# Token mixer on Trainium2: ranks in two products from a count kept per image, narrower query passes, and the last pair's work in another place

## The chip, the cores and the metric

The kernel runs on one core of one Trainium2 chip. The metric is the device time of one launch in microseconds (us). A core has TensorE (PE; its weight loads are listed as PEld), VectorE (DVE), ScalarE (ACT), GpSimd (POOL) and SyncE (SP), which only issues DMAs. Each runs its own list of instructions in order, and they meet at semaphores.

## The reference, cut to what matters

```python
h = tok(x)                               # 64 images of 3x96x96: 36 patches of 768 numbers -> 256, a class token, positions
h = concatenate([h, txt], axis=1)        # 64 x 114 x 256
# linear attention, 16 heads of 16, no softmax
n = layernorm(h); Q, K, V = n@Wq.T+bq, n@Wk.T+bk, n@Wv.T+bv
Q, K = elu(Q)+1, elu(K)+1
KV = einsum('bshd,bshe->bhde', K, V);  Z = 1/(Q . sum_s K + 1e-6)
h = h + einsum('bshd,bhde,bsh->bshe', Q, KV, Z) @ Wo.T + bo
# top-1 mixture of 8 experts
x = layernorm(h); logits = x @ gate_w.T; sel = argmax(logits); rw = sigmoid(max(logits))
xs = x * rw                              # only the chosen expert e = sel works on a row
h = h + (xs @ w_up[e].T) * silu(xs @ w_gate[e].T) @ w_down[e].T
```

## The kernel before, in words

**Stages.** A start of about 50 us makes the patch rows. Then comes a loop over 32 pairs of images (a pair is two images of 114 tokens, `p` is the pair, `i` the step), in which each engine works on several pairs at once: in step i TensorE makes keys, values and queries of pair i, applies the attention of pair i-1, projects out pair i-2 and ranks pair i-4; VectorE routes pair i-3 and takes the statistics of pair i+2 (`stats_1`) and of pair i-2 (`stats_2`); GpSimd works on the second layer norm of pair i-3 (`rstd2_of`), scatters pair i-4 and works on the first layer norm of pair i+2 (`rstd1_of`). Behind the loop the last pairs are finished among the first tiles of the expert stage: 64 tiles of 128 rows sorted by expert, two at a time (a duo, `Turn(0, m)`, `duo_step`), 32 duos. All orders are written out by hand, in the functions `step` of each engine and in the straight lists behind the loop.

**Numbers in float32.** A product of precise numbers is three passes over a high and a low part of each operand (`product`, lines 1537 to 1539). The query product of a pair is 12 such passes: 2 halves `c` by 2 halves `k` by 3. They are 264 columns wide though only 228 are used, because the bank `b_w` is then seeded with the bias and the 264 columns of the output projection are added on it.

**Ranks.** Every token needs its place in its expert's region. `route` on VectorE makes `chosen`, a 0/1 mask of 114 tokens by 8 experts for each of the two images, and `so_far` holds for each partition the number of choices of all earlier pairs (its last row holds the start of each region). `rank(p)` on TensorE sums with matrices of ones: choices earlier in the image (line 1570), those of the first image for the second (line 1571), and the two halves of `so_far` (line 1573, twice). `count_chosen(p)` on GpSimd adds `chosen` to `so_far`, in two buffers by turns. `rank(p)` thus needs the count up to pair p-1 only. `places` on VectorE masks the ranks, and GpSimd's `scatter` writes the rows, two indirect DMAs a pair, to `sorted_rows`.

**Early table.** Once 23 pairs are counted, TensorE, VectorE and GpSimd work out which expert each of the first 32 tiles has (`early_count`, `early_slots`, `early_ends_out`, `early_share`, and on GpSimd `early_past`, `early_sums`, `early_rows` in steps 28, 29 and 30). The late 32 tiles follow from `late_count` and so on after the last pair.

**GpSimd's queue.** Step i is `rstd2_of(i-3)`, `ids_in(i-3)`, `scatter(i-4)`, `count_chosen(i-3)`, `rstd1_of(i+2)`, `top_value(i-3)`, then in steps 5 to 28 the low part of one expert weight (lines 711 and 716). `scatter` waits for ScalarE's `gains`. ScalarE's `tanh(p)` waits for `top_value(p)`. Behind the loop GpSimd also issues all 64 stores of results (`store`, line 820, one indirect DMA a tile), in the same queue as the last pairs' counts, norms and scatters. A store needs only VectorE's result of its tile (line 1427), and 16 result buffers stand between the two.

Of the kernel before, what the change touches and what calls it, by code (L numbers as in the profile page):

```python
# [115 lines left out]
def build(nc, x, txt, w_tok, pos, wq, bq, wkgv, wo, wo_rows, bias, drop, bias_kv, bo_col, wgu_in, wdown_in, ids, consts, slots, out):  # L116
    scratch = nc.dram_tensor("sorted_rows", (EXPERTS * REGION + P, ROW), F32, kind="Internal").ap()

    with ExitStack() as ctx:
# [515 lines left out]
        def _(pool):  # L635
# [197 lines left out]
            store(Turn(0, 1))  # L833
# [10 lines left out]
        def _(act):  # L844
# [273 lines left out]
        def _(dve):  # L1118
# [157 lines left out]
            def route(p):  # L1276
# [13 lines left out]
                if p >= 2:  # L1290
                    dve.wait_ge(so_far_ready, p - 1)
# [19 lines left out]
            def early_link(ins, count):  # L1311

                ins.then_inc(early_chain, 1)
                dve.wait_ge(early_chain, count)

            def early_count():
# [3 lines left out]
                early_link(V.tensor_scalar(early_i[:, 0:1], early_held, con["c_regcol"][:, 0:1], None, ALU.subtract), 1)  # L1320
                early_link(V.tensor_scalar(early_i[:, 1:2], early_i[:, 0:1], P.bit_length() - 1, None, ALU.logical_shift_right), 2)
# [20 lines left out]
            def step(i):  # L1342
# [6 lines left out]
                if 0 <= i - 4:  # L1349
                    places(i - 4)  # L1350
# [696 lines left out]
```

## Time and profile before

| what | us |
|---|---|
| median of 3 runs (lowest, highest) | 429.08 (428.54, 429.84) |
| the profiled execution, its own time | 429.01 |
| its span, first to last instruction | 427.2 |
| PE busy, weight loads | 403.9, 397.4 |
| DVE, ACT, POOL busy | 353.5, 318.1, 288.1 |
| share of the chain that ended last: PE, POOL | 91%, 2% |
| mean granted TensorE clock | 0.982 of full speed |

The span is the stretch that the profile shows; the launch has 1.8 us around it. "Busy" of an engine is the sum over its instructions. A chain entry gives what the next instruction was waiting for, and where nothing was waited for, the instruction before it on the same engine. A matmul's recorded length overlaps with the next ones, so what one costs is read from the distance of starts or from the lengths in the chain. The rest of this document gives times as us from the span's start.

### The profile page before, as it was taken

What the parts mean: (1) busy time and instruction counts of PE and PEld (TensorE: products, weight loads), DVE (VectorE), ACT (ScalarE), POOL (GpSimd) and SP (SyncE); (2) the same over time, 40 slices, a digit from 0 to 9 for tenths busy, and PEclk for the clock granted to TensorE, in tenths of its full rate; (3) what the DMA queues carried; (4) which work ended last, traced back from release to release, by engine and by line L of the source; (5) the groups of instructions that cost most, each with busy time, mean ns of one, the idle gap of its engine ahead of it and who ended that gap; (6) DMA issues with size and microseconds to landing.
All of it is one profiled execution on the core that took longest, in us unless ns stands there. A gap on an engine that the chain in (4) does not pass through costs nothing.

```text
span 427.2 us, 13531 instructions
## 1 busy us (share of the span) xinstructions
PE 403.9 (95%) x4389; PEld 397.4 (93%) x4389; DVE 353.5 (83%) x1076; ACT 318.1 (74%) x856; POOL 288.1 (67%) x539
## 2 busy tenths in 40 slices
PE   7999999999999999999999999999989999999920
PEld 7999999999999999999999999999989999999910
DVE  5677558999999999999999999998888987777730
ACT  5444477789989988988998898888697877777700
POOL 4065212577788788788878878778757677777772
PEclk9999999999999999999999999999999999999975
DMA  8975121232432131332112112200684469622220
GB/s 282 343 239 165 48 49 48 87 110 71 120 99 66 42 111 51 89 107 57 39 50 61 45 39 64 65 25 24 168 224 144 162 190 295 219 82 90 75 92 15
DMA packets 34151, 46.49 MB, mean 109 GB/s; under 512 B 8842, under 2 KB 25856, under 8 KB 34082
## 3 DMA queue, kind: packets, MB, share of 16 engines
q1 hardware_dynamic: 24860, 30.50, 23.7%
q0 software_dynamic: 9216, 15.12, 11.4%
q8 instruction: 37, 0.61, 0.6%
q14 instruction: 32, 0.26, 0.2%
q10 hardware_dynamic: 6, 0.00, 0.0%
HBM read 26.87 MB, written 17.17 MB: 103 GB/s over the span
## 4 chain that ended last, share of the span: by engine, by line
PE 91%; POOL 2%; issue 2%; DMA 1%; ACT 1%; DVE 1%; POOLq 0%; SPq 0%
PE b_kg L1537 9%; PE b_w L1537 8%; PE b_kg L1539 8%; PE b_kg L1538 8%; PE b_w L1538 8%; PE b_w L1539 8%; PE b_att L1652 7%; PE b_t L1602 4%; PE b_v L1539 3%; PE b_v L1537 3%; PE b_v L1538 3%; PE b_t L1666 3%; PE b_att L1589 3%; PE b_att L1537 3%; PE b_att L1539 2%; PE b_att L1538 2%
## 5 line engine op out<-in xcount | busy, mean ns | idle before, releaser
L702 POOL DMA_INDIRECT sorted_rows<-rows,place x64 | 75.1, 1174 | 41.7 <-ACT rows L887 29.5
L820 POOL DMA_INDIRECT out<-result,rows_all x64 | 66.5, 1039 | 20.2 <-issue 13.1
L956 ACT ACTIVATE q_exp<-b_w,bq_s 128x228 f32<-128x228 f32 x64 | 28.9, 452 | 24.4 <-PE b_w L1539 24.4
L1537 PE MATMUL b_w<-xnT_hi,wq_hi 128*128 128x264 f32 x128 | 39.5, 309 | 0.1
L1537 PE MATMUL b_kg<-wkgv_hi,xnT_hi 128*114 128x264 f32 x128 | 38.7, 302 | 0.4 <-DVE patch_out L1164 0.4
L1063 ACT ACTIVATE silu_g<-b_kg,rows_all 128x128 f32<-128x128 f32 x64 | 23.5, 368 | 20.6 <-PE b_kg L1539 18.7
L1537 PE MATMUL b_kg<-wgu_hi,xsT_hi 128*128 x128 | 36.6, 286 | 0.0
L1538 PE MATMUL b_kg<-wkgv_lo,xnT_hi 128*114 128x264 f32 x128 | 36.4, 285 | 0.0
L1538 PE MATMUL b_w<-xnT_lo,wq_hi 128*128 128x264 f32 x128 | 36.4, 285 | 0.0
L1539 PE MATMUL b_kg<-wkgv_hi,xnT_lo 128*114 128x264 f32 x128 | 36.4, 284 | 0.0
L1539 PE MATMUL b_w<-xnT_hi,wq_lo 128*128 128x264 f32 x128 | 36.4, 284 | 0.0
L1652 PE MATMUL b_att<-kv_sb,qT 128*114 128x136 f32 x256 | 34.9, 279 | 1.3 <-DVE qT L1226 1.3
L1539 PE MATMUL b_v<-wkgv_hi,xnT_lo 128*114 128x256 f32 x128 | 36.1, 282 | 0.0
L1537 PE MATMUL b_v<-wkgv_hi,xnT_hi 128*114 128x256 f32 x128 | 36.0, 281 | 0.0
L1538 PE MATMUL b_kg<-wgu_lo,xsT_hi 128*128 x128 | 35.8, 280 | 0.0
L1538 PE MATMUL b_v<-wkgv_lo,xnT_hi 128*114 128x256 f32 x128 | 35.7, 279 | 0.0
L1538 PE MATMUL b_w<-wo_lo,attnT_hi 128*114 128x264 f32 x124 | 35.2, 284 | 0.0
L1537 PE MATMUL b_w<-wo_hi,attnT_hi 128*114 128x264 f32 x124 | 35.1, 283 | 0.0
L1539 PE MATMUL b_w<-wo_hi,attnT_lo 128*114 128x264 f32 x124 | 35.1, 283 | 0.0
L911 ACT ACTIVATE xn<-rows_all,shift,rstd 114x255 f32<-114x255 f32 x64 | 34.8, 595 | 0.0
L1652 PEld LDWEIGHTS b_att<-kv_sb,qT 128*114 128x114 f32 x256 | 31.7, 178 | 1.5 <-issue 1.5
L901 ACT ACTIVATE rows<-rows,mean_neg 114x256 f32<-114x256 f32 x64 | 29.2, 510 | 0.1
(250 smaller groups left out, 1640.6 us busy)
## 6 DMA issues: line engine op xcount, KB each, us to landing
rows_all<-sorted_rows SPq DMA_DIRECT2D x64, 130.0 KB
rows_all<-in_x SPq DMA_DIRECT2D x18, 384.0 KB, 4.8
rows_all<-in_txt SPq DMA_DIRECT2D x32, 154.0 KB
rows_all<-in_wgu_in SPq DMA_DIRECT2D x8, 256.0 KB, 2.9
rows_all<-patch_out SPq DMA_DIRECT2D x48, 36.0 KB
sorted_rows<-tail_rows SPq DMA_DIRECT2D x9, 130.0 KB, 2.3
sorted_rows<-rows,place POOLq DMA_INDIRECT x64, 3.8
rows_all<-in_wdown_in SPq DMA_DIRECT2D x2, 512.0 KB, 4.6
```

The lines of the kernel that those rows point to most:

```text
L702: G.indirect_dma_start(out=scratch[0:EXPERTS * REGION, :], out_offset=bass.IndirectOffsetOnAxis(ap=place[:, k, b:b + 1], axis=0), in_=rows ...
L820: G.indirect_dma_start(out=out, out_offset=bass.IndirectOffsetOnAxis(ap=rows_all[:, t.n, ID:ID + 1].bitcast(I32), axis=0), in_=result[:, k ...
L901: last = S.activation(rows[:, p % 4, b, 0:D], rows[:, p % 4, b, 0:D], ACT.Identity, bias=mean_neg[:, b:b + 1])
L911: last = S.activation(xn[:, b, 1:], rows_all[0:TOK, 2 * p + b, 1:D], ACT.Identity, bias=shift1[:, p % 8, b:b + 1], scale=rstd1[:, p % 8, b ...
L956: S.activation(q_exp[:, c, :], at, ACT.Exp, bias=bq_s[:, c:c + 1])
L1063: S.activation(silu_g[:, t.slot(4)], bank[:, 0:INNER], ACT.Silu, scale=gain)
L1537: T.matmul(to, left_hi, right_hi, start=start, stop=False, skip_group_check=seeded)
L1538: T.matmul(to, left_hi, right_lo, start=False, stop=False, skip_group_check=seeded)
L1539: return T.matmul(to, left_lo, right_hi, start=False, stop=stop, skip_group_check=seeded)
L1589: last = T.matmul(b_kv[j * PART:(j + 1) * PART, b * KC + c], k_sb[:, b, at:at + PART], v_sb[:, b, c, j, :], start=True, stop=True)
L1602: last = T.transpose(turn_attn_bank(p)[:, at:at + TOK], attn[:, b, c * P:(c + 1) * P], ident[0:TOK, 0:TOK])
L1652: last = T.matmul(b_att[0:TOK, b, c * KVW:(c + 1) * KVW], qT[:, c, b * TOK:(b + 1) * TOK], kv_sb[:, b * KC + c].rearrange("p j w -> p (j w ...
```

## The change

1. `so_far` now holds two running numbers of each expert: the count before the pair, and the count with its first image. `count_chosen(p)` on GpSimd makes the second and then, waiting for it, the count for the next pair: two additions of 8 columns in place of one of 16. `rank(p)` is two products in place of four, and waits for the first addition of its own pair. The products of `early_count` and `late_count` are one in place of two. The constant that fills `so_far` at the start now holds the region starts in both halves.
2. GpSimd's step has another order: norms of both kinds first, then the tile table's last part, the count, the scatter, `top_value`.
3. Ten of the twelve query passes of a pair are 256 columns wide in place of 264.
4. VectorE's small chain for the early table is spread over its step, so that other work stands between its links.
5. Behind the loop: ScalarE takes `tanh` and `gains` of pairs 28, 29 and 31 earlier (and the last pair's ahead of duo 5); VectorE takes `stats_2(31)` ahead of duo 3, not behind duo 4; GpSimd's `scatter(31)` stands ahead of the stores of duo 2, and `rstd2_of(31)` ahead of those of duo 1.

```diff
# gpsimd
             def count_chosen(p):
                 pool.wait_ge(chosen_ready, p + 1)
                 if p >= 1:
+                    pool.wait_ge(so_far_ready, 2 * p)
                     pool.wait_ge(rank_done, p)
-                    pool.wait_ge(so_far_ready, p)
-                G.tensor_tensor(so_far[0:TOK, (p + 1) % 2], so_far[0:TOK, p % 2], chosen[:, p % 2],
-                                ALU.add).then_inc(so_far_ready, 1)
+                now, then = so_far[0:TOK, p % 2], so_far[0:TOK, (p + 1) % 2]
+                G.tensor_tensor(now[:, 1], now[:, 0], chosen[:, p % 2, 0], ALU.add).then_inc(so_far_ready, 1)
+                pool.wait_ge(so_far_ready, 2 * p + 1)
+                G.tensor_tensor(then[:, 0], now[:, 1], chosen[:, p % 2, 1], ALU.add).then_inc(so_far_ready, 1)
...
             def step(i):
+                if 0 <= i - 3:
+                    rstd2_of(i - 3)
+                    ids_in(i - 3)
+                if 0 <= i + 2 < PAIRS:
+                    rstd1_of(i + 2)
                 if i == EARLY_PAIRS + 7:
                     early_rows()
                 if 0 <= i - 3:
-                    rstd2_of(i - 3)
-                    ids_in(i - 3)
+                    count_chosen(i - 3)
                 if 0 <= i - 4:
                     scatter(i - 4)
-                if 0 <= i - 3:
-                    count_chosen(i - 3)
-                if 0 <= i + 2 < PAIRS:
-                    rstd1_of(i + 2)
                 if 0 <= i - 3:
                     top_value(i - 3)
...
             scatter(PAIRS - 2)
-            store(Turn(0, 1))
             rstd2_of(PAIRS - 1)
             ids_in(PAIRS - 1)
             top_value(PAIRS - 1)
-            store(Turn(0, 2))
+            store(Turn(0, 1))
             scatter(PAIRS - 1)
-            for m in range(3, DUOS):
+            for m in range(2, DUOS):
                 store(Turn(0, m))
# scalar, behind the loop
             attention_high(PAIRS - 2)
+            tanh(PAIRS - 4)
             seed_bias(PAIRS - 2)
+            gains(PAIRS - 4)
             rows_high(Turn(0, 0))
-            tanh(PAIRS - 4)
             means(PAIRS - 3)
-            gains(PAIRS - 4)
...
             rows_high(Turn(0, 1))
+            tanh(PAIRS - 3)
             attention_high(PAIRS - 1)
-            tanh(PAIRS - 3)
+            gains(PAIRS - 3)
             gate_and_up(Turn(0, 0))
-            gains(PAIRS - 3)
...
             duo_step(Turn(0, 4))
-            duo_step(Turn(0, 5))
+            tanh(PAIRS - 1)
             means(PAIRS - 1)
             centred(PAIRS - 1)
-            duo_step(Turn(0, 6))
-            tanh(PAIRS - 1)
             gains(PAIRS - 1)
-            straight(range(7, DUOS + 1), duo_step)
+            straight(range(5, DUOS + 1), duo_step)
# vector
+                if i == EARLY_PAIRS + 4:
+                    early_whole()
+                if i == EARLY_PAIRS + 5:
+                    early_share()
                 if 0 <= i - 2:
                     attention_low(i - 2)
-                if i == EARLY_PAIRS + 5:
-                    early_share()
+                if i == EARLY_PAIRS + 4:
+                    early_number()
                 if 0 <= i - 1:
                     queries(i - 1)
+                if i == EARLY_PAIRS + 5:
+                    early_compare()
...
             places(PAIRS - 1)
+            stats_2(PAIRS - 1)
             duo_step(Turn(0, 3))
             late_count()
             duo_step(Turn(0, 4))
             late_ends()
-            stats_2(PAIRS - 1)
# tensor
             def rank(p):
                 pe.wait_ge(chosen_ready, p + 1)
-                if p >= 1:
-                    pe.wait_ge(so_far_ready, p)
+                pe.wait_ge(so_far_ready, 2 * p + 1)
...
                 T.matmul(ranks, earlier[:], chosen[:, p % 2].rearrange("p b e -> p (b e)"), start=True, stop=False)
-                T.matmul(ranks[:, EXPERTS:], ones_bf[0:TOK, :], chosen[:, p % 2, 0, :], start=False, stop=False)
-                for b in range(2):
-                    last = T.matmul(ranks, ones_bf[:, :], so_far[:, p % 2, b:b + 1, :].to_broadcast([P, 2, EXPERTS]),
-                                    start=False, stop=(b == 1))
-                last.then_inc(rank_done, 1)
+                T.matmul(ranks, ones_bf[:, :], so_far[:, p % 2].rearrange("p b e -> p (b e)"), start=False, stop=True).then_inc(rank_done, 1)
...
             def queries(p):
                         w = slice(c * P, (c + 1) * P)
-                        last = product(b_w[:, c, 0:QW], (wq_hi[:, k, w], wq_lo[:, k, w]),
-                                       (xnT_hi[:, p % 2, k, :], xnT_lo[:, p % 2, k, :]), k == 0, k == KC - 1)
+                        width = QW if k == 0 else D
+                        T.matmul(b_w[:, c, 0:width], wq_hi[:, k, w], xnT_hi[:, p % 2, k, 0:width], start=(k == 0), stop=False,
+                                 skip_group_check=True)
+                        T.matmul(b_w[:, c, 0:D], wq_hi[:, k, w], xnT_lo[:, p % 2, k, 0:D], start=False, stop=False, skip_group_check=True)
+                        last = T.matmul(b_w[:, c, 0:D], wq_lo[:, k, w], xnT_hi[:, p % 2, k, 0:D], start=False, stop=(k == KC - 1),
+                                        skip_group_check=True)
```

## Rows read from the trace of the kernel before

**Rows 1.** Windows: twenty steps of the pair loop (us; busy us by engine).
```profile
100.19:265.20 165.01, 165.01 (x2003) 163.62 (x2002) 154.83 (x521) 145.40 (x401) 130.46 (x281) 1.00 0.24 70
```

**Rows 2.** Waits of VectorE, 100 to 300 us (total, times, longest).
```profile
DVE z L1262 <- ACT den L939: 5.6, 22, 0.3
```

**Rows 3.** Timeline of GpSimd, one step (start, length, instruction, idle before it).
```profile
200.71 0.22 POOL L685 TENSOR_TENSOR so_far<-so_far,chosen 114x16 bf16<-114x16 bf16 x1
...
202.79 0.74 POOL L711 TENSOR_TENSOR wgu_lo<-rows_all,wgu_hi 128x256 fp32r<-128x256 f32 x1
...
204.66 0.58 POOL L669 TENSOR_TENSOR ratio<-spread,rstd_half 114x2 f32<-114x2 f32 x1
...
206.29 1.24 POOL L702 DMA_INDIRECT sorted_rows<-rows,place  x1 [0.93 <-ACT rows L887]
```

**Rows 4.** Timelines, last pair: GpSimd with its first stores; VectorE's results of duo 3.
```profile
324.58 1.06 POOL L820 DMA_INDIRECT out<-result,rows_all  x1 [0.75 <-DVE result L1427]
...
334.77 0.27 POOL L664 TENSOR_SCALAR ve<-rows 114x2 f32<-114x2 f32 x1 [2.08 <-DVE rows L1182]
...
342.55 1.00 POOL L820 DMA_INDIRECT out<-result,rows_all  x1 [0.30 <-issue]
...
335.24 0.86 DVE L1427 SCALAR_TENSOR_TENSOR result<-rows_all,b_att 128x256 f32<-128x256 f32 x2
```

**Rows 5.** Timelines, expert stage: VectorE's result of duo 23 and a gate product; GpSimd's stores.
```profile
390.49 0.87 DVE L1427 SCALAR_TENSOR_TENSOR result<-rows_all,b_att 128x256 f32<-128x256 f32 x2
...
395.29 0.43 DVE L1411 TENSOR_TENSOR act_u<-up_g,silu_g 128x256 f32<-128x256 f32 x1 [0.59 <-ACT up_g L1064]
...
395.37 1.20 POOL L820 DMA_INDIRECT out<-result,rows_all  x1 [0.30 <-issue]
396.87 0.97 POOL L820 DMA_INDIRECT out<-result,rows_all  x1 [0.30 <-DVE result L1427]
```

**Rows 6.** Timelines, the end: VectorE's last results, GpSimd's last store.
```profile
408.97 0.87 DVE L1427 SCALAR_TENSOR_TENSOR result<-rows_all,b_att 128x256 f32<-128x256 f32 x2 [0.24 <-PE b_att L1539]
...
419.22 0.98 POOL L820 DMA_INDIRECT out<-result,rows_all  x1 [0.31 <-issue]
```

**Rows 7.** Chain of waits, 200 to 208.4 us: start us, length us, engine and line.
```profile
200.69 0.12 PE b_w L1538
...
202.02 0.04 PE b_att L1570
202.06 0.05 PE b_att L1571
202.11 0.11 PE b_att L1573 x2
...
204.62 0.12 PE b_v L1537
...
206.04 0.12 PE b_w L1537
```

**Rows 8.** Timeline of VectorE, same step.
```profile
204.56 0.62 DVE L1226 SCALAR_TENSOR_TENSOR qT<-q_exp,q_relu 128x456 f32<-128x456 f32 x1
...
205.88 0.25 DVE L1182 BATCH_NORM_AGGREGATE mv<-stats 114x2 f32<-114x6 f32 x2
```

**Rows 9.** Timeline of all engines, 305.2 to 305.9 us: GpSimd's power under VectorE's mask.
```profile
305.60 0.73 POOL L666 TENSOR_TENSOR rstd_half<-ve,half_neg 114x2 f32<-114x2 f32 x1
...
305.70 0.17 DVE L1293 TENSOR_TENSOR chosen<-ranked,first 114x16 bf16<-114x16 f32 x1
```

**Rows 10.** Timeline of TensorE, last step of the loop: the rank of pair 27.
```profile
301.67 0.17 PE L1570 MATMUL b_att<-chosen,earlier 114*114 114x16 bf16 x1
```

**Rows 11.** Timelines behind the loop: VectorE, ScalarE, TensorE.
```profile
313.50 0.17 DVE L1293 TENSOR_TENSOR chosen<-ranked,first 114x16 bf16<-114x16 f32 x1
...
317.60 0.36 ACT L1063 ACTIVATE silu_g<-b_kg,rows_all 128x128 f32<-128x128 f32 x1
...
319.30 0.44 PE L1814 MATMUL b_w<-con_s,act_u 128*128 128x128 f32 x2
```

More of the change, by code:

```diff
@@ L1290, in route @@
                 if p >= 2:
-                    dve.wait_ge(so_far_ready, p - 1)
+                    dve.wait_ge(so_far_ready, 2 * (p - 1))
                     dve.wait_ge(rank_done, p - 1)
@@ L1309, in places @@
                     V.tensor_reduce(place[:, p % 4, :], place_e[:], AX_X, ALU.add).then_inc(place_ready, 1)
-            def early_link(ins, count):
-                ins.then_inc(early_chain, 1)
-                dve.wait_ge(early_chain, count)
             def early_count():
@@ L1319, in early_count, with early_whole, early_number @@
                 dve.wait_ge(kvm_done, EARLY_PAIRS + 4)
-                early_link(V.tensor_scalar(early_i[:, 0:1], early_held, con["c_regcol"][:, 0:1], None, ALU.subtract), 1)
-                early_link(V.tensor_scalar(early_i[:, 1:2], early_i[:, 0:1], P.bit_length() - 1, None, ALU.logical_shift_right), 2)
-                early_link(V.tensor_copy(early_f[:, 0:1], early_i[:, 1:2]), 3)
+                V.tensor_scalar(early_i[:, 0:1], early_held, con["c_regcol"][:, 0:1], None, ALU.subtract).then_inc(early_chain, 1)
+            def early_whole():
+                dve.wait_ge(early_chain, 1)
+                V.tensor_scalar(early_i[:, 1:2], early_i[:, 0:1], P.bit_length() - 1, None, ALU.logical_shift_right).then_inc(early_chain, 1)
+            def early_number():
+                dve.wait_ge(early_chain, 2)
+                V.tensor_copy(early_f[:, 0:1], early_i[:, 1:2]).then_inc(early_chain, 1)
             def early_ends_out():
@@ L1334, in early_share, with early_compare @@
                 V.scalar_tensor_tensor(early_f[:, 2:3], early_f[:, 1:2], 0.0, early_f[:, 0:1], ALU.max, ALU.min).then_inc(early_chain, 1)
+            def early_compare():
                 dve.wait_ge(early_ends_ready, 1)
@@ L1679, in queries @@
                         w = slice(c * P, (c + 1) * P)
-                        last = product(b_w[:, c, 0:QW], (wq_hi[:, k, w], wq_lo[:, k, w]),
-                                       (xnT_hi[:, p % 2, k, :], xnT_lo[:, p % 2, k, :]), k == 0, k == KC - 1)
+                        width = QW if k == 0 else D
[4 more added lines that the diff above has]
+                                        skip_group_check=True)
                 last.then_inc(q_done, 1)
             def early_count():
-                pe.wait_ge(so_far_ready, EARLY_PAIRS)
+                pe.wait_ge(so_far_ready, 2 * EARLY_PAIRS)
                 pe.wait_ge(attn_ready, EARLY_PAIRS + 3)
-                for b in range(2):
-                    last = T.matmul(early_held, so_far[:, EARLY_PAIRS % 2, b, :], ones_bf[:, 0:1], start=(b == 0), stop=(b == 1))
-                last.then_inc(early_pe, 1)
+                T.matmul(early_held, so_far[:, EARLY_PAIRS % 2, 0, :], ones_bf[:, 0:1], start=True, stop=True).then_inc(early_pe, 1)
             def early_slots():
@@ L1870, in late_count @@
             def late_count():
-                pe.wait_ge(so_far_ready, PAIRS)
-                for b in range(2):
-                    T.matmul(region_ends, ones_bf[:, 0:1], so_far[:, PAIRS % 2, b, :], start=(b == 0), stop=(b == 1))
-                for b in range(2):
-                    last = T.matmul(region_end, so_far[:, PAIRS % 2, b, :], ones_bf[:, 0:1], start=(b == 0), stop=(b == 1))
-                last.then_inc(table_pe, 1)
+                pe.wait_ge(so_far_ready, 2 * PAIRS)
+                T.matmul(region_ends, ones_bf[:, 0:1], so_far[:, PAIRS % 2, 0, :], start=True, stop=True)
+                T.matmul(region_end, so_far[:, PAIRS % 2, 0, :], ones_bf[:, 0:1], start=True, stop=True).then_inc(table_pe, 1)
             def late_slots():
@@ L1931, in constants @@
     region = np.zeros((P, 2 * EXPERTS), f)
-    region[TOK, 0:EXPERTS] = e * REGION
+    region[TOK] = np.tile(e * REGION, 2)
     tables = {
```

## The prediction

> **What bounds the kernel now.** I read the page first: TensorE is busy for 403.9 of 427.2 us and has 91% of the chain. Then the windows of the pair loop: TensorE has no gap in twenty steps, and a step takes 165.01 / 20 = 8.25 us [rows 1]. VectorE waits once a step, 5.6 / 22 = 0.25 us for ScalarE's denominators, which come behind TensorE [rows 2]: its own work is about 8.0 us a step. GpSimd's timeline of a step shows one idle stretch, 0.93 us ahead of the first scatter, for ScalarE's `gains` [rows 3]. An idle time of 0.30 stands ahead of every indirect DMA, and by the other scatters I take twice that as the cost without a wait, so its own work is near 7.94. TensorE leads, but VectorE has 0.25 and GpSimd 0.3 us to spare: the reader is to see that 0.15 us off TensorE's step uses up half of both.
>
> The second thing to see is the end. Every store from 342.55 us on follows the one before with 0.30 us between, the issue time of such a DMA, though for some a result is named as releaser [rows 4, 5]. VectorE's last results end at 408.97 + 0.87 = 409.84, while the last store is issued at 419.22 [rows 6]. The chain of waits turns to TensorE ahead of 405 us because it follows such a named releaser. GpSimd's queue ends the kernel, some nine us behind the results. So every term has to be asked twice: what it does to TensorE's path, and what it does to GpSimd's queue of stores.
>
> **Ranks, TensorE.** In the chain line 1571 takes 0.05 us, line 1573 0.11 for two, so the two products that go are 0.05 + 0.055 = 0.105 us a pair [rows 7]. At 32 pairs that is 3.4 us; I take 3.2, because the first of the remaining ones may expose more of its weight load (bounds 2.6 and 3.4). The Trainium skill, "TensorE: Matmul & The Clock Gate", section Back-to-back issue gap, gives products of up to 64 columns about 25 ns each, by which the 64 products would save 1.6 us; the row shows twice that, and the row decides.
>
> **Query passes.** Eleven passes of 264 columns go from 200.69 to 202.02, 121 ns each; twelve of 256 from 204.62 to 206.04, 118 ns [rows 7]. Single starts in the timeline put the query passes at up to 124 ns. Ten passes a pair by 3 to 6 ns by 32 pairs is 0.8 to 1.9 us; I take 4 ns, 1.3 us. The first pass of each half stays wide.
>
> **Early and late counts.** Three products fewer, and VectorE's chain spread out. Steps 27 and 28 of the timeline are longer than the others by this work, partly since VectorE comes late behind its chain. I give 0.2 us (0 to 0.5).
>
> **The new count on GpSimd.** One addition of 0.22 us [rows 3] that waits for the one before: with its distance 0.3 us a step. GpSimd's work would be 7.94 + 0.3 = 8.24, above the new step of 8.25 - 0.14 = 8.11. But 0.38 of the old 7.94 is a collision: `ratio` starts at 204.66 just behind VectorE's `qT` (204.56, 0.62 long) and takes 0.58 [rows 3, 8], where elsewhere it takes 0.20. Without it the work is 7.86 us. Where such a collision falls in the new order can't be read off; a start anywhere in the 0.62 us pays what is left of them. At 0.25 a step GpSimd just keeps pace, and it can drift until it starts near the end of `qT`, where the cost is small. I cost it at nothing for TensorE, hidden by the slack; with the cover gone it costs up to 0.62 us less 0.25 a step.
>
> The new order puts `rstd1_of` ahead of the count and the scatters; it goes from 0.19 behind the count at 200.71 to the `top_value` just before 202.79, some 1.74 us [rows 3]. It waits for statistics that end at 206.13 [rows 8]; behind it come the count (to 208.4), the two scatters (3.3 us), `top_value` (211.9) and the weight part (212.6), where it ended at 202.79 + 0.74 + 8.25 = 211.8 in the old order. The rank of that pair comes at 202.02 + 8.11 = 210.1 [rows 7]: 1.7 us to spare behind the count. ScalarE's `tanh` of that pair follows `top_value` by some 0.6 us, so it isn't late either. ScalarE's `gains` is long done when the scatter comes, so the old wait is gone.
>
> The Trainium skill, "SBUF — State Buffer", section Who interferes with whom, says that a VectorE instruction with two SBUF inputs and a GpSimd instruction that reads SBUF exclude each other, and that whichever is first holds the port to its end. The `ratio` row agrees for VectorE first. For GpSimd first, a 0.73 us power at 305.60 did not lengthen VectorE's mask at 305.70 (0.17 us) [rows 9], which is against it; a long streaming GpSimd instruction under `qT` isn't in this trace. A rival below is made of that.
>
> **Steps 29 to 31.** GpSimd also makes the tile table, and TensorE ranks pair 27 at 301.67 [rows 10]. New: that rank needs the first addition of pair 27, which stands behind both norms and the table. An estimate from the lengths of these pieces is 301.6 to 301.9 for it: a wait of 0.25 us (0 to 1.0).
>
> **Behind the loop.** The count of pair 29 now stands ahead of the scatter of pair 28, and needs `chosen` at 313.67. So scatter starts near 314.6, not 314.13, `top_value(29)` ends at 317.5, and ScalarE, which now does `tanh(29)` and `gains(29)` ahead of `gate_and_up(0)`, reaches that near 318.6, not 317.60 [rows 11]. TensorE's first `turn_act` came at 319.30, directly behind the product of VectorE that waits for it: no slack, so all of it shows. TensorE's path loses 1.05 us (0 to 1.1).
>
> Sum of TensorE's path: -3.2 - 1.3 - 0.2 + 0.25 + 1.05 = -3.4 us at the last result.
>
> **GpSimd's queue of stores.** Its first store waited 0.75 us for a result, so it moves with TensorE's path: by about -3.4 (the last rank is still to come). From there the queue is full but for one wait, 2.08 us for the last pair's statistics at 334.77 [rows 4]. With `stats_2(31)` ahead of duo 3, these end near 330.2 on the old clock, before GpSimd has scattered pair 30: the wait goes. It pays 0.3 for the second addition. `scatter(31)` ahead of duo 2's stores is an exchange of order inside the queue; it needs `gains(31)`, near 335.2, and comes at 336.5. The two DMAs that it issues are counted in the queue either way. The late tiles' loads still wait for VectorE's table. So duo 3's first store comes at about 342.55 - 3.4 - 1.8 = 337.3.
>
> Duo 3's first result ended at 335.24 + 0.43, so its store was 6.9 us late; new, 5.1. What follows isn't a plain shift: two stores at (0.97 + 0.30) need 2.55 us a duo, and still the queue stopped catching up. Duo 23's first result ended at 390.49 + 0.43 and its store began at 396.87, 6.0 us late [rows 5]; TensorE gives a duo in 2.76 (the distance of its gate products in the timeline). The store at 395.37 starts 0.08 us behind VectorE's gate product, which reads two SBUF tiles, and takes 1.20 where its neighbour takes 0.97: GpSimd gains 0.21 a duo until a store runs into that product, and is then held in step. Either store of a duo can be the held one, so it can stick at 6.0, 4.5 or 3.2 us. From 5.1 it sticks at 4.5, some duos earlier than before. That leaves 6.0 - 4.5 = 1.5 us on top of the path's shift.
>
> Total: -3.4 - 1.5 = -4.9. The results then end at 406.4 and the last store is issued near 414.3 [rows 6], so GpSimd's queue still ends the kernel. From the profiled 429.01 that is 424.1; the median shown, 429.08, is 0.07 higher, which I leave out. ScalarE's block of `tanh`, `means`, `centred` and `gains` (2.1 us) ahead of duo 5 delays the gate products by some 1.2 us; TensorE's `turn_act(5)` has about 1.2, the queue behind it more, so nothing.
>
> **The rivals.**
> - *The engines beside TensorE hold the loop.* For it: 8.24 with an average collision, 8.0 for VectorE. Against: the collision can move. If steps 5 to 28 end at 8.2 in place of 8.11, 24 x 0.09 = 2.2 us of the 4.5 are lost: 426.3, at worst 427.5.
> - *No loss behind the loop.* If `gate_and_up(0)` isn't late (`top_value(29)` comes sooner) and the rank of pair 27 doesn't wait, 1.3 us come back, and the queue sticks at 3.2 rather than 4.5: 424.1 - 1.3 - 1.0 = 421.8, with only half of it 423.
> - *Slower: VectorE and GpSimd lock each other.* If GpSimd's weight part (0.74 us) begins just ahead of `qT`, holds it, and its next instruction is then held by `qT` for 0.5 us, GpSimd's round is 7.86 + 0.5 = 8.36 or more, and VectorE goes with it. It decides from 8.25 on: above, each of 24 steps costs. At 8.36: 24 x 0.11 = 2.6 us more in the loop, with 8 other steps saving 1.1 and the queue 1.5, less 1.3 lost behind the loop: 430.3. The last part of the time table above (weight part to 212.6, `qT` at 212.66) shows how near it is; [rows 9] speak against it. By the port rule of the Trainium skill's page "SBUF — State Buffer" it would go this way.
> - *Not done as said*: if the Q passes gain nothing and the held store doesn't move, the path gives -3.4 + 1.3 = -2.1, which is 426.9. It shares the second case's chance.
>
> **How the numbers follow.** Forecast 0.55 (423.0 to 425.6); the loop held by others or the gains absent 0.2; no loss behind the loop 0.15; locked and slower 0.06; 0.04 for something unnamed. A measurement can tell about 0.3%, 1.3 us, from no change: faster is below 427.8. The forecast, the third case and most of the second are there: 0.88. Same 0.06, slower 0.06. The range takes in the first, second and third cases: 421.8 to 427.0.
>
> **What would show it.** Right: steps of 8.10 to 8.12 us in the windows; no line 1571; GpSimd's scatter without a wait for `gains`, and its first-norm `ve` waiting a little or not at all for statistics; a wait of TensorE near the first `turn_act`; no 2 us wait of GpSimd in the last pair's norm; stores held in step about 4.5 us behind their results. Wrong: steps of 8.2 or more with TensorE or VectorE waiting, `qT` longer than 0.62, a rank that waits for `so_far`, or a last store that moves by no more than the last result.

## The result, and the profile after

The changed kernel takes 431.12 us (430.34 to 432.39), the kernel before 429.08 (428.25 to 430.29): a ratio of 1.0051, with a 95% interval of 1.0029 to 1.0073. The change made it slower by 0.5%, where 424.1 us was forecast. The profiled execution of the changed kernel took 432.39 us with a span of 430.6; that of before had 427.2. It is the slowest of the seven, 1.3 us above their median: what is read from the traces below adds up to 3.4 us, where the medians are 2.0 apart, and where the other runs save that 1.3 us isn't known.

The head of the page after (busy times, then the chain by engine):

```profile
PE 405.8 (94%) x4322; PEld 395.8 (92%) x4322; DVE 355.5 (83%) x1076; ACT 316.9 (74%) x856; POOL 295.4 (69%) x571
...
PE 78%; POOL 6%; issue 5%; DVE 5%; DMA 3%; ACT 2%; POOLq 0%; SPq 0%; DVEq 0%; ACTq 0%
```

TensorE has 67 matmul records fewer and is busy for longer. The chain has left it for 22% of the span, where it was 9%. A window of sixteen steps of the loop, from one `apply` to another:

```profile
133.59:265.57 131.98, 131.98 (x1571) 129.02 (x1570) 124.70 (x417) 115.57 (x322) 105.84 (x241) 1.00 0.22 64
```

131.98 / 16 = 8.25 us a step, as before [rows 1]. The products are gone, the time is not. The column of TensorE says 131.98 of 131.98 and is no proof of work: a matmul's end is modelled, and a wait of 0.1 us hides in it. It is seen in starts. One step of the links from query passes to logits, from the timelines of TensorE, ScalarE and VectorE, first after, then before. (`b_t<-con_s,xn` are the token transposes ahead of the passes; ScalarE makes `q_exp` and `q_relu` of the passes' result, then `attnT_hi`, the high part of the turned attention output; VectorE makes its low part `attnT_lo`, the query `qT` of `q_exp` and `q_relu`, and in the end the logits.)

```profile
200.80 0.39 PE L1687 MATMUL b_w<-xnT_hi,wq_hi 128*128 128x264 f32 x1
202.53 0.45 ACT L957 ACTIVATE q_exp<-b_w,bq_s 128x228 f32<-128x228 f32 x1 [0.72 <-PE b_w L1690]
203.88 0.56 ACT L863 CAST attnT_hi<-b_t 128x456 fp32r<-128x456 f32 x1
204.47 0.63 DVE L1122 TENSOR_TENSOR attnT_lo<-b_t,attnT_hi 128x456 fp32r<-128x456 f32 x1
205.02 0.66 DVE L1225 SCALAR_TENSOR_TENSOR qT<-q_exp,q_relu 128x456 f32<-128x456 f32 x1
208.58 0.56 PE L1672 MATMUL b_t<-con_s,xn 114*128 114x114 f32 x4
208.64 0.35 DVE L1247 SCALAR_TENSOR_TENSOR logits<-b_w,rstd,gate_part 114x8 f32<-114x8 f32 x2
209.05 0.39 PE L1687 MATMUL b_w<-xnT_hi,wq_hi 128*128 128x264 f32 x1
```

```profile
200.30 0.39 PE L1537 MATMUL b_w<-xnT_hi,wq_hi 128*128 128x264 f32 x1
202.06 0.45 ACT L956 ACTIVATE q_exp<-b_w,bq_s 128x228 f32<-128x228 f32 x1 [0.65 <-PE b_w L1539]
203.41 0.56 ACT L862 CAST attnT_hi<-b_t 128x456 fp32r<-128x456 f32 x1
204.02 0.62 DVE L1123 TENSOR_TENSOR attnT_lo<-b_t,attnT_hi 128x456 fp32r<-128x456 f32 x1
208.16 0.35 DVE L1248 SCALAR_TENSOR_TENSOR logits<-b_w,rstd,gate_part 114x8 f32<-114x8 f32 x2
208.25 0.56 PE L1666 MATMUL b_t<-con_s,xn 114*128 114x114 f32 x4
208.57 0.38 PE L1537 MATMUL b_w<-xnT_hi,wq_hi 128*128 128x264 f32 x1
```

The query passes need the logits of the pair before (`logits_ready`) and start 0.06 us after their end, in both kernels. The loop closes: passes, `q_exp` and `q_relu`, `attnT_hi`, `attnT_lo`, then VectorE's order down to the logits, then the next passes. The ranks lie on none of its links. That this round takes one step (8.25 us after, 8.27 in this step of before) is so of every round; what tells is where it has something to spare. The distance from the first of the four token transposes to the passes is 0.32 us in every step of before from 141 to 240 us, and the same in three kernels of the experiments (the query passes, GpSimd's order and the moves behind the loop, each alone): there TensorE goes straight on, and the logits come just in time. In the changed kernel it is 0.47 here and 0.46 on the mean: TensorE waits for the logits.

GpSimd, the same step after (compare [rows 3]), and its groups with VectorE's `qT`, 108 to 265 us, after and then before (busy, mean ns of one, idle). `wgu_lo` is the low part of an expert weight, and `ve` the first instruction of a layer norm:

```profile
200.38 0.20 POOL L686 TENSOR_TENSOR so_far<-so_far,chosen 114x8 bf16<-114x8 bf16 x1
200.66 0.20 POOL L688 TENSOR_TENSOR so_far<-so_far,chosen 114x8 bf16<-114x8 bf16 x1
201.60 1.24 POOL L704 DMA_INDIRECT sorted_rows<-rows,place  x1 [0.74 <-issue]
...
204.43 0.75 POOL L713 TENSOR_TENSOR wgu_lo<-rows_all,wgu_hi 128x256 fp32r<-128x256 f32 x1
205.27 0.47 POOL L664 TENSOR_SCALAR ve<-rows 114x2 f32<-114x2 f32 x1
...
208.63 0.20 POOL L686 TENSOR_TENSOR so_far<-so_far,chosen 114x8 bf16<-114x8 bf16 x1
...
L1225 DVE SCALAR_TENSOR_TENSOR qT<-q_exp,q_relu 128x456 f32<-128x456 f32 x19 | 12.5, 657 | 0.0
L664 POOL TENSOR_SCALAR ve<-rows 114x2 f32<-114x2 f32 x19 | 9.1, 478 | 1.6
```

```profile
L1226 DVE SCALAR_TENSOR_TENSOR qT<-q_exp,q_relu 128x456 f32<-128x456 f32 x19 | 11.8, 623 | 0.0
L664 POOL TENSOR_SCALAR ve<-rows 114x2 f32<-114x2 f32 x19 | 3.7, 193 | 1.6
```

GpSimd's round is 208.63 - 200.38 = 8.25 us with no wait for anyone in it; the 0.74 ahead of the scatter is its issue. `wgu_lo` now ends 0.16 us into `qT`, which takes 0.657 us in place of 0.623, and the `ve` behind it, which ends 0.06 us after `qT`, takes 0.285 us more than before.

Then the last steps, in the timelines of TensorE, ScalarE and VectorE:

```profile
303.01 0.19 PE L1580 MATMUL b_att<-chosen,earlier 114*114 114x16 bf16 x1 [0.74 <-POOL so_far L686]
307.23 0.20 ACT L881 ACTIVATE tanh_top<-top_n 114x2 f32<-114x2 f32 x1 [1.97 <-POOL top_n L677]
308.21 0.69 DVE L1232 SCALAR_TENSOR_TENSOR k_sb<-k_exp,b_kg 114x512 f32<-114x512 f32 x1 [1.35 <-ACT k_exp L924]
317.73 0.35 DVE L1261 RECIPROCAL z<-den 114x32 f32<-114x32 f32 x1 [1.79 <-ACT den L940]
```

The rank of pair 27 [rows 10] waits for the count; `tanh` waits for GpSimd's `top_n` (0.78 us before), and behind it ScalarE makes the keys late, then VectorE. The end, VectorE and GpSimd:

```profile
413.58 0.87 DVE L1438 SCALAR_TENSOR_TENSOR result<-rows_all,b_att 128x256 f32<-128x256 f32 x2 [0.25 <-PE b_att L1550]
422.58 0.98 POOL L822 DMA_INDIRECT out<-result,rows_all  x1 [0.30 <-issue]
```

Results end 4.6 us later than before, stores 3.4 [rows 6]. Where the difference arose, from `attnT_hi` of the same pair in both traces (changed minus before): -0.1 us at the 80th us; +0.35 at the 105th, gained in two steps of 8.39 and 8.61 us; +0.5 at the 270th; 0 at the 278th, where the early counts save their 0.46; +0.6 at the 287th, where it is given back in a wait for logits; +1.5 at the 312th, +3.8 at the 320th; +4.2 at the first `silu`, +4.6 at the last result, less 1.25 that the store queue caught up.

### The profile page after: what moved, and what is told of

Same layout as the page of the kernel before. It is cut to its first block, busy times and chain, and to the rows that moved or that the text cites. A ratio compares the mean times of both kernels' runs of the same rounds, so it can differ in the third digit from the quotient of the medians.

```text
span 430.6 us, 13429 instructions
## 1 busy us (share of the span) xinstructions
PE 405.8 (94%) x4322; PEld 395.8 (92%) x4322; DVE 355.5 (83%) x1076; ACT 316.9 (74%) x856; POOL 295.4 (69%) x571
## 4 chain that ended last, share of the span: by engine, by line
PE 78%; POOL 6%; issue 5%; DVE 5%; DMA 3%; ACT 2%; POOLq 0%; SPq 0%; DVEq 0%; ACTq 0%
PE b_kg L1548 8%; PE b_kg L1549 7%; PE b_kg L1550 7%; PE b_att L1658 6%; PE b_w L1687 4%; PE b_w L1548 4%; PE b_w L1549 4%; PE b_w L1550 4%; PE b_w L1689 3%; PE b_w L1690 3%; PE b_t L1608 3%; PE b_v L1550 3%; PE b_v L1548 3%; PE b_att L1595 3%; PE b_v L1549 3%
## 5 line engine op out<-in xcount | busy, mean ns | idle before, releaser
L1687 PE MATMUL b_w<-xnT_hi,wq_hi 128*128 128x264 f32 (+1 forms) x128 | 39.5, 309 | 1.3 <-DVE logits L1247 1.2
L1658 PE MATMUL b_att<-kv_sb,qT 128*114 128x136 f32 x256 | 35.9, 284 | 2.1 <-issue 2.1
L1689 PE MATMUL b_w<-xnT_lo,wq_hi 128*128 128x256 f32 x128 | 36.0, 281 | 0.0
L1690 PE MATMUL b_w<-xnT_hi,wq_lo 128*128 128x256 f32 x128 | 35.9, 280 | 0.0
```

Source lines behind the costliest of these rows:

```text
L1658: last = T.matmul(b_att[0:TOK, b, c * KVW:(c + 1) * KVW], qT[:, c, b * TOK:(b + 1) * TOK], kv_sb[:, b * KC + c].rearrange("p j w -> p (j w ...
L1687: T.matmul(b_w[:, c, 0:width], wq_hi[:, k, w], xnT_hi[:, p % 2, k, 0:width], start=(k == 0), stop=False, skip_group_check=True)
L1689: T.matmul(b_w[:, c, 0:D], wq_hi[:, k, w], xnT_lo[:, p % 2, k, 0:D], start=False, stop=False, skip_group_check=True)
L1690: last = T.matmul(b_w[:, c, 0:D], wq_lo[:, k, w], xnT_hi[:, p % 2, k, 0:D], start=False, stop=(k == KC - 1), skip_group_check=True)
```

## The experiments

A "step" below is the mean distance of ScalarE's `attnT_hi` over eleven steps near 145 to 237 us: 8.245 us before, 8.248 in the changed kernel. What earlier runs had taught was known when the later expectations were written. All runs do the whole computation; the two with an extra copy add work that nothing uses. Times are medians, and the traces, as above, single executions.

**Parts alone.** The first four put one part of the diff each into the kernel before.

Query passes:

```
- product(b_w[:, c, 0:QW], ..., k == 0, k == KC - 1)
+ width = QW if k == 0 else D      # the diff's three products, nothing else
```

> The kernel before with one edit: the twelve products of the query passes are 256 columns wide instead of 264 (but for the first of each half). Theory A (a cycle holds the loop: query passes on TensorE wait for VectorE's logits of the pair before, which wait for attnT_lo, which waits through ScalarE for the query passes): TensorE's shorter passes shorten one link of the cycle by 0.04 us a step at most, and the steps of the loop stay at 8.25 us within 0.03; the time is 428.2 to 429.3 us. Theory B (the prediction's: TensorE's own sum sets the step): every step is 0.04 us shorter, the time is 1.3 us down, 427.8 us.

427.96 us, ratio 0.9981 (0.9969 to 0.9993); step 8.218. The start of the ranks moves from 1.563 to 1.535 us behind that of the passes: the twelve passes got 0.028 us shorter, the predicted kind and two thirds of the size. It comes out whole, as it shortens a link of the cycle and TensorE alike; the distance ahead of the passes stays at 0.32 us. The time fell by 0.95 us, between both theories.

Ranks:

```
- T.matmul(ranks[:, EXPERTS:], ones_bf[0:TOK, :], chosen[:, p % 2, 0, :], ...) and 2 x (ones_bf, so_far)
+ T.matmul(ranks, ones_bf[:, :], so_far[:, p % 2].rearrange("p b e -> p (b e)"), ...)   # GpSimd: two sums, at the old place
```

> The kernel before with one part of the change: the ranks in two products, with the two sums of GpSimd a pair at their old place behind the scatter, and the counts of the table in fewer products. Theory A (the cycle through VectorE's logits holds the loop): the rank's products lie between the query passes and key_value, on no link of the cycle, so the steps stay at 8.25 us and TensorE gets a gap of 0.1 us a step ahead of the query passes; the time is within 0.5 us of 429.1. Theory B (TensorE's own sum): 0.105 us a step less, 3.2 us down in all, 425.9 us.

433.0 us, ratio 1.0094 (1.0070 to 1.0117): both theories missed a loss. The loop lies between them, nearer to theory A. From the start of the passes to `key_value` it takes 1.727 us in place of 1.825, so the products did save 0.10 us; the distance from the last token transposes to the next passes grew from 0.325 to 0.390, and the step is 8.216: of 0.10 us, 0.03 came out. 8.216 us is thus what the cycle takes when TensorE no longer sets the pace. The loss is at the end, in steps of 10.96 and 10.03 us. TensorE's timeline of this kernel:

```profile
304.19 0.19 PE L1571 MATMUL b_att<-chosen,earlier 114*114 114x16 bf16 x1 [3.01 <-issue]
```

It waits 3.01 us for the first sum of pair 27, which GpSimd ends at 304.1, behind the table's rows and two scatters. Before, the rank asked only for the sum of the pair before.

GpSimd's order:

```
+ rstd2_of(i-3); ids_in(i-3); rstd1_of(i+2); early_rows(); count_chosen(i-3); scatter(i-4); top_value(i-3)
```

> The kernel before with GpSimd's new order of a step alone: rstd2, ids, rstd1, then the table's rows, the count (one sum a pair, as before), the scatter, top_value. Theory A (the loss of the changed kernel in pairs 5 to 8 and in steps 28 to 31 comes of what GpSimd does at other times now): this alone makes the kernel slower by 0.5 to 2.5 us, with the table ended later than the 299.38 us of before, the ranks of the last pairs later, and k_exp of pair 31 later than 305.3 us. Theory B (the order is harmless; the extra sum a pair is what makes GpSimd late): same time as before within 0.4 us, and rank(27) at its old 301.7 us.

429.65 us, ratio 1.0009 (0.9996 to 1.0021). Alone it costs nothing that is clear of noise: step 8.232, but steps of 8.37, 8.42 and, with the table's rows, 8.51 us. The rank of pair 27 comes at 302.26, 0.6 us later than before, of which 0.4 was there from the start of the loop. Neither theory is decided.

Behind the loop:

```
  # GpSimd: rstd2, ids, top_value of pair 31 and its scatter ahead of duo 1's and duo 2's stores
  # ScalarE: tanh/gains of pairs 28, 29, 31 earlier;  VectorE: stats_2(31) ahead of duo 3
```

> The kernel before with the moves behind the loop alone: ScalarE's tanh and gains of pairs 28, 29 and 31 earlier, VectorE's statistics of pair 31 two duos earlier, GpSimd's chain and scatter of pair 31 ahead of the stores of duos 1 and 2. Theory A (prediction's terms for this part): first product of the experts up to 0.9 us later because ScalarE's gains and tanh stand ahead of it, the GpSimd queue freed of its wait of 2.08 us, store lag in duo 23 at 4.5 us instead of 6.0; together 428.2 to 429.3 us. Theory B (the delay of 4 us behind the loop in the changed kernel comes of these moves, not of what comes late out of the loop): slower by 2 to 4 us, 431 to 433 us, with the first silu of the experts 3 us or more behind its old 317.60 us.

427.38 us, ratio 0.9959 (0.9944 to 0.9973). Its results end 0.8 us later than before, of which its loop had 0.5 from the start (`attnT_hi` at 80.21 against 79.67), and its last store is issued at 417.49, 1.7 us earlier: the store queue's part of the prediction is there. It is faster than theory A's range, and theory B is out. The expectation's lag of 4.5 us was wrong: the stores settle 3.1 to 3.2 us behind their results (5.9 before, 4.4 in the changed kernel), the lowest of the three levels that the prediction named.

**Parts together, and the cycle.** The changed kernel with GpSimd's old order:

> The changed kernel with GpSimd's old order of a step (the two sums of the count behind the scatter). Known so far: the ranks alone took a step of the loop from 8.245 to 8.215 us, the narrower query passes alone to 8.215 us too, and the ranks alone lost 5.5 us in the last steps, where TensorE waited for the count. Theory A (what is won on TensorE in the loop is given back by GpSimd's new order, whose subtraction of the expert weights' low parts comes to lie ahead of VectorE's qT): step of 8.18 to 8.20 us and qT at 0.624 us, against 8.25 and 0.657 in the changed kernel; the end of the loop then loses as in the ranks-alone kernel, 430 to 431.5 us in all. Theory B (VectorE's links of the cycle set 8.21 to 8.25 us whatever GpSimd's order): step at 8.21 us or more; 431 to 432.5 us.

430.62 us, ratio 1.0040 (1.0026 to 1.0055); step 8.178, `qT` 0.62 us; rank(27) waits 3.03 us. Theory A: in the old order the two savings on TensorE give 0.067 us a step. Of 0.13 us saved, the other half stands ahead of the passes (0.388 in place of 0.325).

VectorE's `stats_1` out of the stretch from `attnT_lo` to the logits, in the kernel before and in the changed one:

```
  def step(i):
+     stats_1(i + 2)               # inside it, one more wait: for its own result of the pair before
      masked(i - 1)
      ...
      queries(i - 1)
-     stats_1(i + 2)
      route(i - 3)
```

> The kernel before with one edit on VectorE: stats_1(i + 2) stands at the start of its step, ahead of masked(i - 1), and no longer between qT and route; nothing is left out. Theory A (cycle through the logits that TensorE's query passes wait for, with statistics of 0.95 us in its stretch from attnT_lo to the logits): the logits come up to 0.9 us earlier against TensorE's query passes, whose wait goes, and the step falls from 8.245 to TensorE's own sum, 8.15 to 8.22 us: 1 to 3 us faster. Theory B (TensorE's own sum is 8.24 us, no wait ahead of the query passes): no change within 0.4 us. Theory C (the order costs on ScalarE's or GpSimd's side, as attnT_lo or the chain of the variances comes later): slower by over 0.5 us.

429.36 us, ratio 1.0003 (0.9991 to 1.0015). Theory B: steps of 8.24 (one of 8.45, not followed). With 0.95 us less in the cycle the step stays: in the kernel before TensorE's own sum sets it, 8.24 us, and the cycle, 8.216 by the kernel with the ranks alone, is only 0.03 us behind.

> The changed kernel with the same edit, stats_1(i + 2) at the start of VectorE's step. Theory A (cycle through the logits): the step falls from 8.25 to the larger of VectorE's own sum (7.80 us busy and 0.34 us of its short waits) and TensorE's, 8.10 to 8.16 us, some 2.5 to 4 us less in all: 427.5 to 428.7 us. Theory B (VectorE's whole in-order sum with its waits already is 8.25 us): no change, 431.1 us within 0.5. The losses of pairs 28 to 31, behind GpSimd, stay in both.

427.27 us, ratio 0.9963 (0.9948 to 0.9977), 3.8 us below the changed kernel and below theory A's range, so theory B is out; steps of 8.08 to 8.17, and one of 8.46. The steps of 8.4 to 8.6 near 100 us are gone too. This one edit takes 0.95 us from the cycle and moves `qT` away from `wgu_lo` at once, so it doesn't say which of the two held the loop at 8.25.

**GpSimd, three times.** The table's rows behind the count, the scatter and `top_value`, in the changed kernel:

> The changed kernel with one edit on GpSimd: in the step of pair 30's projections the six small operations that make the first table's rows (1.9 us) stand behind the count, the scatter and top_value, not ahead of them. Theory A (the late count of pair 27 and late top_value behind these rows stall TensorE and VectorE in the last steps): rank(27) at 301.3 to 301.9 us instead of 303.01, steps 28 to 31 shorter by 1 to 3 us, the last result earlier by as much unless the table, now 3 us or so later, is waited for by the loads of the sorted rows; 428.5 to 430 us. Theory B (GpSimd is late by its whole work of those steps, whatever the place): no gain or a loss from the later table, 431 to 433 us.

429.98 us, ratio 1.0036 (1.0018 to 1.0055): 1.1 us off, in theory A's range. rank(27) comes at 302.10 in place of 303.01, the last three steps are together 1.8 us shorter, and the table, ended near 306.7, is not missed by TensorE.

The extra copy (in the changed kernel; one profiled execution):

```
+ if 12 <= i < EARLY_PAIRS:
+     G.tensor_copy(idle_out[:], idle_in[:])      # 114 x 16
  top_value(i - 3)
```

> The changed kernel with one more GpSimd operation in each of the steps 12 to 22 of the loop, ahead of top_value: a copy of 114x16 elements between two tiles that nothing else uses, 0.2 us and some 0.08 us of issue. Theory A (GpSimd has slack in the loop of the changed kernel, and the cycle over VectorE's logits sets 8.25 us): these steps stay at 8.25 us within 0.05. Theory B (GpSimd's own queue is full and sets the step of the changed kernel): each of the eleven steps takes 0.2 to 0.3 us more, 8.45 to 8.55 us, some 3 us in all.

432.47 us; the eleven steps take 92.0 / 11 = 8.36 us and those on either side 8.21 to 8.25. 0.17 us more on GpSimd (the distance to the next start) cost 0.12 us of every step, which speaks for theory B, at half its size. Its rows:

```profile
191.96 0.20 POOL L688 TENSOR_TENSOR so_far<-so_far,chosen 114x8 bf16<-114x8 bf16 x1
...
196.16 0.73 POOL L715 TENSOR_TENSOR wgu_lo<-rows_all,wgu_hi 128x256 fp32r<-128x256 f32 x1
...
200.31 0.20 POOL L688 TENSOR_TENSOR so_far<-so_far,chosen 114x8 bf16<-114x8 bf16 x1
...
204.50 0.74 POOL L715 TENSOR_TENSOR wgu_lo<-rows_all,wgu_hi 128x256 fp32r<-128x256 f32 x1
204.96 0.78 DVE L1230 SCALAR_TENSOR_TENSOR qT<-q_exp,q_relu 128x456 f32<-128x456 f32 x1
```

`wgu_lo` has slid 0.12 us further into `qT`, which takes 0.78 us here and 0.773 on the mean, 0.12 more than 0.657. That is how a GpSimd that nobody waits for sets the pace: the later it is, the more it stretches `qT`, until VectorE is as slow as GpSimd.

`wgu_lo` moved out of `qT`'s way, in the changed kernel:

```
  rstd2_of(i - 3); ids_in(i - 3)
+ gate_up_low(...)        # of the step before; stood last in its step
  rstd1_of(i + 2)
```

> The changed kernel with one edit on GpSimd: the subtraction that makes wgu_lo of a step (0.74 us, steps 5 to 20) stands some 1.3 us later, behind rstd2 and the ids of the next step and ahead of rstd1, so that it lies beside VectorE's statistics and no longer ahead of qT. Theory A (the loop of the changed kernel is set by GpSimd's full queue, 7.97 us of its own and 0.27 us that VectorE's qT holds of the operation behind wgu_lo): with qT out of the way qT takes 0.62 us and these steps 8.17 to 8.20 us, as with the old order; 1 us or so off in all. If the chain of rstd2 now meets qT instead (its power operation held), the step stays above 8.2. Theory B (the new order costs the loop by what it does to other engines' waits, wherever wgu_lo stands): 8.25 us a step.

430.36 us, ratio 1.0053 (1.0035 to 1.0071). The steps say theory A: 8.18 us and `qT` 0.62 with GpSimd's same work in nearly the same order, so it isn't the order as such that cost the loop. The whole time doesn't show the expected 1 us: its ratio is that of the changed kernel. Steps of 8.4 and 8.6 us near 100 us and the loss of steps 28 to 31 are all still there.

**A version that keeps the gains.** GpSimd's old order, but from pair 30's step on the count ahead of the scatter:

```
+ if i >= EARLY_PAIRS + 7:
+     count_chosen(i - 3)
  scatter(i - 4)
- count_chosen(i - 3)
+ if 0 <= i - 3 < EARLY_PAIRS + 4:
+     count_chosen(i - 3)
```

With the ranks alone:

> The kernel before with the ranks in two products and GpSimd's old order, as in the ranks-alone kernel, but from the step of pair 30 on the count of a pair stands ahead of the scatter. Theory A (the ranks alone lost 5.5 us because in the last steps TensorE waited up to 3 us for a count that stood behind two indirect stores of 1.5 us each and behind the table's rows): rank(27) waits under 0.3 us, steps 28 to 31 go back to some 8.2 us, and 0.03 us a step of the loop is left: 427.8 to 428.8 us. Theory B (GpSimd's whole work of those steps is too much once a second sum is in it): at least 2 us of the loss stay, 431 us or more.

429.24 us, ratio 1.0008 (0.9998 to 1.0018). No wait of 3 us; 3.8 us come back, so theory B is out, though it is 0.4 us above theory A's range. But the ranks by themselves then are worth nothing that can be measured.

With all the rest of the change:

> The changed kernel with GpSimd's old order of a step up to pair 29's, and from pair 30's on the count ahead of the scatter. Steps of the loop as in the old-order kernel, 8.18 us. Theory A (as above): no long wait for a count at the end; against before 0.065 us x 24 steps less and the 1.5 us of the moves behind the loop: 425.5 to 426.7 us. Theory B: some 430 us.

426.90 us, ratio 0.9960 (0.9947 to 0.9973), a little above the range. GpSimd's count of pair 27 and TensorE's rank in this kernel:

```profile
298.44 0.20 POOL L686 TENSOR_TENSOR so_far<-so_far,chosen 114x8 bf16<-114x8 bf16 x1
298.94 0.17 PE L1582 MATMUL b_att<-chosen,earlier 114*114 114x16 bf16 x1
```

The extra copy in this one:

> The kernel with GpSimd's old order and the count ahead of the scatter from pair 30's step on, with the same extra copy of 114x16 elements in each of the steps 12 to 22. In the changed kernel this copy took 0.12 us a step. Theory A (in the old order GpSimd waits 0.3 us and more a step for ScalarE's gains ahead of the scatter, which keeps it in step with the loop, and the extra copy is taken from that wait): steps 12 to 22 stay at 8.18 us within 0.02. Theory B (any GpSimd operation beyond what the kernel before had costs the loop): 8.25 us or more in these steps.

426.80 us, ratio 0.9963 (0.9950 to 0.9976); steps of 8.17, so the copy costs nothing where GpSimd has a wait to take it from. Its rows of the scatter:

```profile
168.83 0.20 POOL L765 COPY idle_out<-idle_in 114x16 f32<-114x16 f32 x1
...
172.13 1.24 POOL L706 DMA_INDIRECT sorted_rows<-rows,place  x1 [0.81 <-ACT rows L895]
```

And with `stats_1` first in VectorE's step:

> The same kernel with VectorE's stats_1(i + 2) at the start of its step. Theory A (the cycle query passes - ScalarE - attnT_lo - logits sets 8.18 us; 0.95 us of VectorE leave its stretch): step falls to the next bound, TensorE's sum of 8.10 or VectorE's of 8.13 us: 1 to 2 us less than its neighbour without the edit, 424 to 425.5 us. Theory B (what the same edit won on the changed kernel, 3.8 us, came from taking VectorE's qT out of the way of GpSimd's subtraction, which the old order has done already): no further gain, within 0.5 us of the neighbour.

425.88 us, ratio 0.9926 (0.9907 to 0.9945): the best, below both kernels. Most steps are 8.08 or 8.17 to 8.2, with one of 8.46. Against its neighbour it is 1.0 us, at the edge of what the intervals tell apart (in the profiled executions 22 steps of the loop take 179.35 us against 180.14); it lies between the theories, the bound of 8.10 isn't reached, and what holds the longer of the steps was not followed.

## Why the prediction was wrong

- *Ranks, -3.2 us, and query passes, -1.3 us.* The prices were right for TensorE's ranks (0.10 us a pair against 0.105) and near for the passes (0.028 against 0.04). **The step that failed is the one ahead of them: that beside TensorE's sum VectorE has 0.25 us to spare and GpSimd 0.3.** TensorE did lead, but by 0.03 us: the cycle through VectorE's logits takes 8.216 us. The 0.25 of [rows 2] is a wait inside VectorE's order, not slack of the cycle that runs through it: the query passes already started 0.06 us behind the logits. In the old order the cycle keeps back half of what TensorE saves: 8.178 us a step in place of 8.11. I had read each engine's idle time and never followed one pair's `logits_ready` round to the next.
- *The new count, hidden.* This took the other half. GpSimd's own round is 8.25 - 0.285 = 7.97 us, not 7.86, mostly since the issue ahead of the first scatter takes 0.74 us behind the count, where I had 0.6; the collision I let fall "where the cost is small" settled at `qT`, because it is pulled there. This is the rival of the lock, to which I gave 0.06. Its mechanism, place and sign were right; it came at 8.25 us, not 8.36, as `ve` is held for 0.285 us and not 0.5. Moving `wgu_lo` (8.18) and the copy in both orders (+0.12, 0) show it. That the step came out just as long as before, 8.25, is chance. [rows 9], which I let speak against it, show a power of two elements a row, not a streaming subtraction. By the rule in the Trainium skill, "SBUF — State Buffer", section Who interferes with whom, that whichever of two such instructions is first keeps the other out, it was to be expected; the traces agree for `wgu_lo` (0.12 us more of overlap made `qT` 0.12 us longer) and for the `ve` behind it, not for the powers (last section).
- *Steps 29 to 31, +0.25 us (0 to 1.0).* Measured 3.2 us in the trace. The wait of rank(27), 0.74 us, is inside the bounds. What I left out is `top_value` behind the table's rows and the scatters: I had worked out its lateness for a plain step (none) and not for the one with 1.9 us of rows in it. Then `tanh` waited 1.97 us (0.78 before), and with it everything behind on ScalarE. The kernel with the rows last got 1.1 us back; the one with the old order and the count ahead of the scatter loses 0.6 us in these steps.
- *Early counts, -0.2 us.* They did save 0.46 (a step of 8.33 us in place of 8.79). The changed kernel gave back all of it in the next step, in a wait for the logits (9.15 in place of 8.58); with GpSimd's old order that step is 8.65 to 8.68, and most of the saving stays.
- *Behind the loop, +1.05 us.* Right in kind: +0.8 from `attnT_hi` of the last pair to the last result in the changed kernel, but +0.4 in the part alone, which is the better measure of it.
- *Stores, -1.5 us.* Right, 1.25 in the trace. The 2.08 us wait is gone, and the store held by VectorE's product is now the one that begins 4.5 us behind its duo's first result (399.98 against 395.10 + 0.43), where it was 6.0 [rows 5]. The kernel with the moves alone shows it as a gain.

Together, in the traces: the loop up to 287 us +0.6 in place of -4 and more, the last steps +3.2 in place of +0.25, behind them +0.8 in place of +1.05, the stores -1.25 in place of -1.5; that is the 3.4 us between the spans.

Open: why two steps of 8.4 and 8.6 us come near 100 us in the changed kernel and three of its variants, and not in those with `stats_1` moved or with GpSimd's old order (in the changed kernel's, VectorE waits 0.48 us for TensorE's key-value products and the next passes 0.29 for the logits); where one step of 8.45 to 8.47 near 200 us comes from in all three kernels with `stats_1` first; and what bounds the loop at 8.15 us in the best version.

## What to carry to other kernels

An engine without a gap may lead by next to nothing: follow one item from its product through the other engines back to the product of the next item, in starts, and compare the length of that round with the engine's sum. A saving counts beyond that lead only if it is on the round and on the engine. An engine that nobody waits for can still set the pace by stretching another engine's instruction, once its queue has no wait left to absorb a late start; so a second instruction there is free or not free depending on whether its round still contains a wait. And where a reader's dependence moves from the item before to this item, check the steps in which the writer has extra work, not the average one.

## What the runs showed of the hardware

Where GpSimd's subtraction of 128x256 ran 0.16 us into VectorE's `qT`, which reads two SBUF tiles, `qT` took 0.657 us in place of 0.623; where it ran 0.28 us into it, 0.773 (kernel with the extra copy). The GpSimd operation of two elements a row behind it took 0.478 us in place of 0.193.

GpSimd's power of two elements a row is another case. In all the traces here `qT` began 0.04 to 0.69 us after the start of such a power 243 times: the power took 0.69 to 0.73 us and `qT` 0.61 to 0.64, so neither held the other. Once it began closer behind, and the power was held. The kernel with `wgu_lo` moved, then the changed kernel, timelines of GpSimd and VectorE:

```profile
187.16 0.72 POOL L666 TENSOR_TENSOR rstd_half<-ve,half_neg 114x2 f32<-114x2 f32 x1
187.25 0.62 DVE L1225 SCALAR_TENSOR_TENSOR qT<-q_exp,q_relu 128x456 f32<-128x456 f32 x1
```

```profile
97.50 1.23 POOL L666 TENSOR_TENSOR rstd_half<-ve,half_neg 114x2 f32<-114x2 f32 x1
97.53 0.62 DVE L1225 SCALAR_TENSOR_TENSOR qT<-q_exp,q_relu 128x456 f32<-128x456 f32 x1
```

Here the power began 0.03 us ahead of `qT` and took 1.23 us in place of 0.72, while `qT` took its usual 0.62. This is one case only; why 0.04 us of lead was enough and 0.03 was not, no run shows.
